# A router that takes four tiles at a time, in a mixture-of-experts kernel that has to be routed first

## The chip, the cores and the metric

The kernel runs on one core of one Trainium2 chip. The metric is the device time of one launch in microseconds (us). The kernel before took 273.12 us as the median of three runs (271.77 to 273.74). The profile shown here is of one further execution.

## The reference, cut to what matters

```python
w = weights[conditions]                      # (32, 64, 64), chosen per sequence
xf = einsum('bct,bcd->bdt', x, w)            # x is (32, 64, 512): 2048 tokens of 512
gate = softmax(xf @ Wr.T)                    # 8 experts
top2_val, top2_idx = top_k(gate, 2)
keep = rank_of_token_within_expert <= 640    # in the order of the tokens
g = silu(xf @ Wg[e].T); u = xf @ Wu[e].T     # 352 wide
y = sum_e comb[:, e] * ((g * u) @ Wd[e].T)
return x + y
```

All tensors are float32. Every token is first mixed with the matrix of its own condition, and then sent to its two best experts, each of which takes at most 640 tokens.

## The kernel before, in words

**Two halves.** The first 42 us find out which token goes to which expert; the rest computes the eight experts. Expert 0 works on tiles of 128 tokens; experts 1 to 7 work on 512 tokens together and on a fifth tile if there is one. Products in the experts are made from a high and a low part of each operand ("high" by ScalarE, `w_high`, `x_high`; "low" by VectorE, `w0_low`, `x_low`).

**The route.** The tokens lie in 16 tiles of 128 (`TT`), in 8 pairs (`NM`), and SyncE (SP) loads a pair with each DMA of 512 KB (`load_x`, L345). The logits are computed as wq^T (x Wr), so the router does not wait for xf. For each tile: TensorE turns four 128x128 blocks of x into one bank (`x_tile_turn`, L1171), VectorE (tiles 1, 2, 5, 6, 9) or ScalarE (the others) copies that bank to a ring of four slots in SBUF, `turned_sb`. For each pair, `router` (L1182) multiplies by Wr, the four blocks of the contraction in four column groups of 32 of the array; VectorE copies the result (`xrT_copy`, L815), TensorE turns it back (`turn`, L1195), and VectorE adds the four parts (`xr_sum`, L820). `logits` (L1210) multiplies by the matrix of the condition, wq, in four groups of tiles, `LG`, of 6, 4, 4 and 2. After each group VectorE finds the two largest of eight (`top_two`, L827). `one_hot` makes the choice a matrix of ones, three small products give each token its rank in its expert (L1269 and L1272), a chain of VectorE steps makes slots of it (L902 to L934), 32 products turn slots into lists of rows (L1283, into `ps_slot`), and VectorE writes the lists (L951, `lists_ok`).

**xf.** `condition(j)` (L1227) computes the rows of xf for a pair, four banks in a ring; ScalarE copies them to `xf_sb` (`xf_copy`, L590), and SP stores each pair to DRAM (L390, L394). Two conditions stand before the last routers, two more before the rank products, four behind them. Then TensorE runs `KEEP_WARM` products whose result nobody reads (L1289).

**The handover.** GpSimd (POOL) gathers the rows of an expert from DRAM by indirect DMA (`gather`, L494). Its first gather waits for `lists_ok` 1 and for `xf_out`, which counts all stores of xf (L485, L486). TensorE turns the gathered tile (`x_turn`, L1296) and starts the first expert (L1385).

**Queues.** SP issues in the order of its text: cond, x pairs 0 and 1, wr, x pairs 2 to 7, two small padding rows, eight `place` DMAs that spread wq (after `wsel_in`), the four gate and up parts of expert 0's weights, the stores of xf, the gates' store, and the down part of expert 0's weights (`load_unit(0, KH)`, L398). Then come the weights of expert 1, each when its part of the buffer is free. The matrices of the other eight tiles come by eight gathers on POOL (L454).

## Time and profile before

| | before |
|---|---|
| median of 3 runs | 273.12 us (271.77 to 273.74) |
| the profiled execution's own time | 272.44 us |
| its span | 270.6 us |
| TensorE busy, whole span | 257.8 us, 95% |
| TensorE busy, 42 to 265 us | 220.3 of 223.0 us |
| VectorE, ScalarE, GpSimd busy | 161.6, 137.7, 173.6 us |
| granted clock of TensorE, mean | 0.991 |
| DMA moved | 59.00 MB |

How to read it: a granted clock of 1.00 is 2.4 GHz, 0.50 is 1.2 GHz. A row of the timeline gives the start of a group of like instructions, how long it lasted from the first start to the last end, and the idle time of its engine before it with what ended that. For an issue on SPq the length is that of the issue, not of the transfer; the landing is a column of the view of DMA issues. A DMA share of 1.00 means that all 16 DMA engines were busy.

### The profile page before, as it was taken

The page shows a single profiled execution, that of the slowest core. Times are in us where ns is not written, and L with a number is a line of the kernel's source. Part 1 is how long each engine was busy: PE and PEld are TensorE (multiplying, and loading weights), DVE is VectorE, ACT ScalarE, POOL GpSimd, SP SyncE. Part 2 cuts the span into 40 slices and gives each one's busy share as a digit, 9 for nine tenths or more (in the row PEclk, how much of TensorE's full clock was granted, in tenths as well). Part 3 has the DMA queues.
Part 4 walks back from the last instruction along what each step waited for, and adds up shares of the span by engine and source line. Part 5 has one row for each costly group of instructions (what it writes and reads, how often), then busy time and mean ns, then how long its engine had stood idle before and what let it go on. Part 6 is the DMA issues. An engine that isn't in the chain of part 4 may idle for free.

```text
span 270.6 us, 4016 instructions
## 1 busy us (share of the span) xinstructions
PE 257.8 (95%) x1368; PEld 200.0 (74%) x1368; DVE 161.6 (60%) x332; ACT 137.7 (51%) x242; POOL 173.6 (64%) x156
## 2 busy tenths in 40 slices
PE   8999698999999999999999999999999999999991
PEld 4663156999987867888878887777787777878980
DVE  2658998444459664876566639674865867343251
ACT  2356843444464656565366644664565559442100
POOL 5792048741158867884887478858887886685742
PEclk9999979999999999999999999999999999999998
DMA  6996888999869998899679867998899699366441
GB/s 201 363 300 241 344 270 272 386 338 330 294 193 209 202 207 256 162 216 277 170 130 250 238 178 111 200 294 251 154 238 329 148 192 225 40 79 81 131 177 46
DMA packets 27099, 59.00 MB, mean 218 GB/s; under 512 B 6198, under 2 KB 6454, under 8 KB 26976
## 3 DMA queue, kind: packets, MB, share of 16 engines
q1 hardware_dynamic: 16416, 37.89, 44.3%
q0 software_dynamic: 10656, 20.75, 37.2%
q8 instruction: 16, 0.26, 0.4%
q14 instruction: 11, 0.09, 0.1%
HBM read 39.56 MB, written 20.25 MB: 221 GB/s over the span
## 4 chain that ended last, share of the span: by engine, by line
PE 52%; DVE 3%; ACT 2%; DMA 2%; issue 2%; POOLq 0%; ACTq 0%; DVEq 0%
PE bank L1342 19%; PE bank L1429 17%; PE bank L1437 9%; PE bank L1316 3%; DMA xg<-xf_dram,src_turn 2%; PE bank L1444 2%; PE bank L1452 2%; DVE w L1005 1%; ACT hhi L696 1%; POOLq L85 0%; DVE squares L1054 0%; PE bank L1303 0%; DVE hlo L1060 0%; DVE h L1120 0%; DVE h_last L1100 0%
## 5 line engine op out<-in xcount | busy, mean ns | idle before, releaser
L1429 PE MATMUL bank<-xhi,w 128*128 128x512 f32 x280 | 71.6, 398 | 0.0
L1342 PE MATMUL bank<-w,hhi 128*128 128x512 f32 (+1 forms) x216 | 67.1, 393 | 1.5 <-ACT y_sb L667 1.0
L554 POOL DMA_INDIRECT out<-y_sb,dst_row x35 | 56.5, 1613 | 13.4 <-issue 13.4
L1429 PEld LDWEIGHTS bank<-xhi,w 128*128 128x128 f32 x280 | 52.3, 188 | 13.2 <-DVE h_last L1100 0.8
L520 POOL DMA_INDIRECT gate_g<-gates_dram,src_row x40 | 46.8, 1170 | 12.1 <-issue 11.5
L1342 PEld LDWEIGHTS bank<-w,hhi 128*128 128x128 f32 x216 | 39.2, 188 | 10.7 <-DVE hlo L1060 1.6
L1005 DVE TENSOR_TENSOR w<-raw,w 128x704 fp32r<-128x704 f32 (+1 forms) x35 | 37.1, 1060 | 14.6 <-ACT w L609 8.2
L508 POOL DMA_INDIRECT xg<-xf_dram,src_turn x24 | 25.6, 1065 | 26.0 <-DVE xlo L990 11.6
L1342 PE MATMUL bank<-w,hlo 128*128 128x512 f32 (+1 forms) x108 | 41.9, 388 | 0.0
L1437 PE MATMUL bank<-xlo,w 128*128 128x512 f32 x140 | 38.4, 396 | 0.0
L609 ACT ACTIVATE w<-raw 128x704 fp32r<-128x704 f32 (+1 forms) x40 | 36.7, 923 | 0.0
L508 POOL DMA_INDIRECT xg<-xf_dram,src_row x16 | 18.1, 1130 | 27.5 <-DMA xf_dram<-xf_sb 15.9
L1054 DVE STREAM_TRANSPOSE squares<-xg 128x512 f32<-128x512 f32 x24 | 24.0, 1046 | 16.7 <-DMA xg<-xf_dram,src_turn 16.7
L1437 PEld LDWEIGHTS bank<-xlo,w 128*128 128x128 f32 x140 | 26.4, 189 | 6.4
L667 ACT ACTIVATE y_sb<-bank,gate_g 128x512 f32<-128x512 f32 x30 | 20.1, 686 | 20.0 <-PE bank L1342 18.6
L1342 PEld LDWEIGHTS bank<-w,hlo 128*128 128x128 f32 x108 | 20.3, 188 | 4.6
L1316 PE MATMUL bank<-w,xhi 128*128 128x352 f32 x112 | 20.5, 327 | 0.8 <-ACT xhi L644 0.8
L1316 PEld LDWEIGHTS bank<-w,xhi 128*128 128x128 f32 x112 | 18.2, 189 | 1.4 <-issue 1.0
L696 ACT ACTIVATE hhi<-h 128x512 fp32r<-128x512 f32 x14 | 8.9, 634 | 19.6 <-DVE h L1107 12.0
L1060 DVE TENSOR_TENSOR hlo<-h,hhi 128x512 fp32r<-128x512 f32 x14 | 9.7, 693 | 10.4 <-ACT hhi L696 10.4
L990 DVE TENSOR_TENSOR xlo<-xg,xhi 128x512 fp32r<-128x512 f32 x24 | 15.0, 684 | 1.5 <-ACT xhi L654 1.5
L654 ACT ACTIVATE xhi<-xg 128x512 fp32r<-128x512 f32 x24 | 13.3, 620 | 2.7 <-DMA xg<-squares 2.7
(138 smaller groups left out, 304.8 us busy)
## 6 DMA issues: line engine op xcount, KB each, us to landing
raw<-wgu SPq DMA_DIRECT2D x32, 352.0 KB, 7.8
xg<-squares SPq DMA_DIRECT2D x24, 256.0 KB, 7.5
x_sb<-x SPq DMA_DIRECT2D x8, 512.0 KB, 7.6
raw<-wd SPq DMA_DIRECT2D x8, 512.0 KB
xf_dram<-xf_sb SPq DMA_DIRECT2D x7, 512.0 KB, 3.0
raw<-wd SPq DMA_DIRECT2D x8, 192.0 KB
out<-x SPq DMA_DIRECT2D x1, 1280.0 KB, 18.3
gate_g<-gates_dram,src_row POOLq DMA_INDIRECT x40, 6.5
```

The lines of the kernel that those rows point to most:

```text
L508: nc.gpsimd.indirect_dma_start(out=xg[:, t, :], out_offset=None, in_=xf_dram[:, :], in_offset=bass.IndirectOffsetOnAxis(ap=rows, axis=0), ...
L520: nc.gpsimd.indirect_dma_start(out=gate_g[:, n % TPE, :], out_offset=None, in_=gates_dram[:, :], in_offset=bass.IndirectOffsetOnAxis(ap=sr ...
L554: nc.gpsimd.indirect_dma_start(out=out[:, :], in_=y_sb[:, n % TPE, :], in_offset=None, out_offset=bass.IndirectOffsetOnAxis(ap=dst_row[:, ...
L609: last = nc.scalar.activation(w[:, half, 0, a:b], raw[:, a:b], ACT.Copy)
L667: nc.scalar.activation(y_sb[:, t, :], y_bank(e, t)[:, :], ACT.Copy, scale=gate_g[:, t, e:e + 1]).then_inc(y_ok, n)
L990: nc.vector.tensor_tensor(xlo4[:, :, cols], turned_rows(e, t), xhi4[:, :, cols].bitcast(F32), ALU.subtract).then_inc(xlo_ok, n)
L1005: last = nc.vector.tensor_tensor(w[:, half, 1, a:b], raw[:, a:b], w[:, half, 0, a:b].bitcast(F32), ALU.subtract)
L1054: nc.vector.transpose(squares[:, :, t, :], xg[:, t, :].rearrange("p (i b) -> p b i", i=SQ)).then_inc(squares_ok, 1)
L1316: last = nc.tensor.matmul(ps[:, 0:I], left[:, b, c], w[:, half, part, o:o + I], start=(k == 0 and left is xhi and part == 0), stop=(k == K ...
L1342: last = nc.tensor.matmul(ps[:, cols], left(c), w[:, half, part, o:o + width], start=(c == 0 and q == 0), stop=(closes and c == cs[-1] and ...
L1429: last = nc.tensor.matmul(ACC_BANK[what][:, :], columns(what, k, part), xhi4[:, k, :], start=(k == 0 and part == 0), stop=False)
L1437: last = nc.tensor.matmul(ACC_BANK[what][:, :], columns(what, k, 0), xlo4[:, k, :], start=False, stop=(k == KH - 1))
```

## The change

The router works on four tiles instead of two (`router(g)`, g 0 to 3), in a ring of twelve slots `turned_x`, with products 512 columns wide; the copies of the results of groups 2 and 3 are made by ScalarE, and group 3 has banks 2 and 3 for itself. The last two tiles of x are loaded a second time, already turned (`xt`, 512 KB, prepared as another input); their blocks are not turned on TensorE, nor copied. x pair 7, needed only for xf, is loaded after the `place` DMAs, and so are the padding rows. The groups of logits are 4, 4, 4 and 4 tiles. All conditions come after the last logits, two ahead of the rank products and six behind. All softmax work is done once, the sums between the slots and the lists, the last product after the lists. The down part of expert 0's weights is loaded ahead of the stores of xf. Its high part is made before `x_high(0)`, its low part before `x_low(0)`; all low parts of gate and up come after the lists; the copies to `src_turn` come after `x_low(0)`. `KEEP_WARM` goes from 18 to 25.

```diff
-LG = ((0, 3), (3, 5), (5, 7), (7, NM))
+LG = ((0, 2), (2, 4), (4, 6), (6, NM))
-KEEP_WARM = 18
+KEEP_WARM = 25
-        ps_xrT, ps_xr = bank[6:8]
+        ps_xrT = (bank[6], bank[6], bank[6], bank[2])
+        ps_xr = (bank[7], bank[7], bank[7], bank[3])
+        XRT_DVE = 2
# SP
-            for m in range(2, NM):
+            for m in range(2, NM - 1):
                 load_x(m)
-            (the two padding rows)
+            sp.dma_start(turned_x[:, RING:RING + 2, :, :], xt...).then_inc(xt_in, 16)
             for j in range(HALF, TT):
                 place(j)
+            load_x(NM - 1)
+            (the two padding rows)
-            for u in range(KH):
+            for u in range(NU):
                 load_unit(0, u)
             (the stores of xf, the store of the gates)
-            load_unit(0, KH)
# ScalarE
-            (xf_copy of 16 tiles, exps after 2 and 6 of them, w_high(0) after 4)
+            for g in range(XRT_DVE, NG):
+                act.wait_ge(xrT_ps, g + 1)
+                nc.scalar.activation(xrT[:, g % 2, :], ps_xrT[g][:, :], ACT.Copy).then_inc(xrT_ok, 1)
+            for n in range(TT):
+                xf_copy(n, n % XR)
+                if n == TT - 3:
+                    act.wait_ge(sub_ok, 2)
+                    nc.scalar.activation(ex[:, :, :], lg[:, :, :], ACT.Exp).then_inc(ex_ok, 1)
+            w_high(KH, 0, 0)
             x_high(0)
-            w_high(KH, 0, 0)
# VectorE
+            for j in TURN_DVE[0:4]:
+                turn_copy(j)
+            xrT_copy(0)
+            for j in TURN_DVE[4:]:
+                turn_copy(j)
+            xrT_copy(1)
+            xr_sum(0)
+            xr_sum(1)
+            top_two(0)
+            top_two(1)
+            xr_sum(2)
             one_hot(0)
+            xr_sum(3)
+            top_two(2, 3)
             subtract(LG[3][0] * 2, TT)
             one_hot(1)
+            subtract(0, LG[3][0] * 2)
...
+            w0_low(KH)
             x_low(0)
-            w0_low(KH)
+            (the 16 copies to src_turn)
# TensorE
             router(g):
+                        for half, r in enumerate((turned_slot(g * XR), RING)):   # g == 3, for each k
+                            cols = slice(half * 2 * P, (half + 1) * 2 * P)
+                            last = nc.tensor.matmul(ps_xrT[g][k * Q:(k + 1) * Q, cols], wr_sb[:, k, :], turned_x[:, r:r + 2, k, :])
+            turn_tiles(0, 8)
+            pe.wait_ge(wr_in, 16)
+            router(0)
+            turn_tiles(8, 12)
+            router(1)
+            turn(0)
+            turn_tiles(12, TURNED)
+            turn(1)
+            logits(0)
+            router(2)
+            logits(1)
+            router(3)
+            turn(2)
+            turn(3)
+            logits(2)
+            logits(3)
+            condition(0)
+            condition(2)
             (the rank products)
-            for j in range(after, TT, 2):
+            for j in range(4, TT, 2):
                 condition(j)
# first expert
-                    pe.wait_ge(wlo0_ok, KH)
+                    pe.wait_ge(wlo0_ok, 2)
...
+                if s == 0:
+                    pe.wait_ge(wlo0_ok, KH)
                 first_gate_up(s, n, (2, 3))
```

## Rows read from the trace of the kernel before

**Rows 1.** Busy time in stretches: start:end, length, engines, granted clock, DMA share, GB/s
```profile
0.00:42.00 42.00, 37.52 (x335) 19.35 (x335) 29.15 (x127) 20.39 (x36) 20.27 (x33) 0.96 0.83 283
42.00:265.00 223.00, 220.32 (x1033) 180.65 (x1033) 132.27 (x206) 117.35 (x206) 152.25 (x123) 1.00 0.83 210
```

**Rows 2.** Waits of TensorE from 78 to 265 us: total, times, longest
```profile
PE bank L1342 <- ACT y_sb L667: 1.0, 1, 1.0
PE bank L1342 <- DVE hlo L1060: 0.5, 1, 0.5
```

**Rows 3.** Timeline at the handover: start, length, engine, line, what, idle before
```profile
37.55 1.73 POOL L508 DMA_INDIRECT xg<-xf_dram,src_row  x1 [15.88 <-DMA xf_dram<-xf_sb]
...
36.08 5.75 PE L1289 MATMUL bank<-iota_q 128*128 128x512 f16 x18
42.09 0.63 PE L1303 MATMUL bank<-ident,xg 128*128 128x128 f32 x4 [0.26 <-DMA xg<-xf_dram,src_row]
43.49 1.50 PE L1316 MATMUL bank<-w,xhi 128*128 128x352 f32 x8 [0.78 <-ACT xhi L644]
```

**Rows 4.** Issues of xf's stores, first and last: timeline, and us from issue to landing
```profile
23.23 0.33 SPq L390 DMA_DIRECT2D xf_dram<-xf_sb  x1
...
xf_dram<-xf_sb SPq DMA_DIRECT2D x1, 512.0 KB, 2.6
...
33.49 0.85 SPq L394 DMA_DIRECT2D xf_dram<-xf_sb  x1
...
xf_dram<-xf_sb SPq DMA_DIRECT2D x1, 256.0 KB, 3.3
```

**Rows 5.** Timeline of VectorE, the route's last steps
```profile
26.86 0.38 DVE L845 TENSOR_TENSOR ohp<-iota_e,i 128x128 bf16<-128x128 f32 x1
27.92 0.70 DVE L902 TENSOR_TENSOR_SCAN run<-carry,bank 128x264 f32<-128x264 f32 x1
36.29 0.20 DVE L951 TENSOR_SCALAR src_row<-bank 128x40 uint32<-128x40 f32 x1
39.92 3.41 DVE L974 COPY src_turn<-src_row 32x6 uint32<-32x6 uint32 x16
```

**Rows 6.** Busy time in stretches, DMA share and GB/s last: loads, idle, stores
```profile
3.00:22.00 19.00, 18.46 (x190) 11.32 (x188) 9.70 (x47) 6.25 (x11) 15.64 (x23) 1.00 1.04 333
22.00:23.00 1.00, 1.00 (x18) 0.42 (x18) 0.86 (x7) 0.88 (x2) 0.00 (x0) 1.00 0.15 59
28.00:30.00 2.00, 1.71 (x16) 0.30 (x8) 1.90 (x4) 1.24 (x4) 0.00 (x0) 1.00 1.00 406
```

**Rows 7.** Timeline of TensorE and VectorE in the router's stretch
```profile
14.59 1.04 PE L1178 MATMUL bank<-ident,x_sb 128*128 128x128 f32 x8
15.56 0.64 PE L1190 MATMUL bank<-turned_sb,wr_sb 128*32 128x256 f32 x8
16.13 0.44 PE L1201 MATMUL bank<-ident,xrT 128*128 128x128 f32 x2
20.73 0.41 PE L1223 MATMUL bank<-xr,wq 64*64 64x8 f32 x16
20.99 1.07 PE L1234 MATMUL bank<-x_sb,wq 64*64 64x512 f32 x8
21.21 0.39 DVE L832 MAX8 v<-bank 128x8 f32<-128x8 f32 x4
...
22.34 0.24 DVE L864 TENSOR_TENSOR lg<-bank,v 128x80 f32<-128x80 f32 x1
```

**Rows 8.** Issue and us to landing of x pair 7, last of the x loads
```profile
5.42 0.64 SPq L348 DMA_DIRECT2D x_sb<-x  x1
...
x_sb<-x SPq DMA_DIRECT2D x1, 512.0 KB, 12.0
```

**Rows 9.** Copies of xf by ScalarE, timeline
```profile
31.40 2.06 ACT L593 ACTIVATE xf_sb<-bank 128x512 f32 x4 [0.32 <-PE bank L1234]
```

**Rows 10.** Busy time and granted clock in the two stretches after 36.8 us
```profile
36.80:40.20 3.40, 3.40 (x10) 1.19 (x9) 3.28 (x10) 0.22 (x2) 2.34 (x2) 0.50 0.70 207
40.20:43.60 3.40, 2.37 (x13) 1.08 (x12) 3.16 (x16) 0.85 (x2) 2.52 (x3) 1.00 0.67 173
```

More of the change, by code:

```diff
@@ L39 @@
 AQ = 8
[L40 to L44 removed]
+LG = ((0, 2), (2, 4), (4, 6), (6, NM))
+NG = len(LG)
+RING = 3 * XR
+TURNED = TT - 2
 WARM_UP = 10
[L47 removed]
+KEEP_WARM = 25
 BASE = TPE - 1
@@ L279, in build, with turned_slot @@
         TURN_DVE = [1, 2, 5, 6, 9]
-        TURN_ACT = [j for j in range(TT) if j not in TURN_DVE]
+        TURN_ACT = [j for j in range(TURNED) if j not in TURN_DVE]
+        def turned_slot(j):
+            return j % RING if j < TURNED else RING + j - TURNED
         def group_of(j):
@@ L943, in w0_low @@
                                         ALU.subtract).then_inc(wlo0_ok, 1)
-            for u in range(W0_EARLY):
-                w0_low(u)
+            gate_sums()
             dve.wait_ge(slot_ps, 1)
@@ L1203, in turn @@
+                last.then_inc(xrT_ps, 1)
+            def turn(g):
+                pe.wait_ge(xrT_ok, g + 1)
+                if 1 <= g < NG - 1:
+                    pe.wait_ge(xr_ok, g)
+                for j in range(XR):
+                    last = nc.tensor.transpose(ps_xr[g][:, j * P:(j + 1) * P],
+                                               xrT[:, g % 2, j * P:(j + 1) * P], ident[:, :])
                 last.then_inc(xr_ps, 1)
```

193 lines of the change are left out of this document (73 added, 120 removed).

## The prediction

> **What bounds the kernel now.** I read the stretches first. From 42 to 265 us TensorE is busy 220.3 of 223.0 us at full clock, and before that only 37.5 of 42 [rows 1]. Its waits in the experts come to 1.5 us in all from 78 us on [rows 2]. The change touches no product of experts 1 to 7. So the end stands at a nearly fixed distance behind the first expert's first tile turn, at 42.09 [rows 3], and the question is what moves that.
>
> The timeline at the handover says who holds it. TensorE's filler products end at 41.83, and the turn waits 0.26 us for a gathered tile; the gather was issued by POOL at 37.55, and POOL had been released by a store of xf [rows 3]. Two things have to be there: the lists, whose first write runs 36.29 to 36.49 [rows 5], and all stores: the last is issued at 33.49 and lands 3.3 us later, at 36.8 [rows 4]. The stores decide, but the lists are only 0.3 us ahead. Whoever makes the route faster alone gains nothing, and whoever makes the stores faster alone gains 0.3 us.
>
> What do the stores hang on? The first is issued at 23.23 and lands in 2.6 us [rows 4]. While they flow freely the 16 DMA engines are full at 406 GB/s, and from 22 to 23 us they are nearly empty, since the loads are through [rows 6]. All of xf is 8 x 524 KB; at 406 GB/s a pair takes 1.29 us and the eight 10.3. The fixed part of a store is 2.6 - 1.3 = 1.3 us. A stream that never runs dry would have landed at 23.23 + 1.3 + 10.3 = 34.9; it landed at 36.8, so 1.9 us were gaps behind ScalarE, whose copies share the time with routers, exps and a weight part.
>
> **The route, part by part.** A tile pair's turns take 1.0 us, a router of 256 columns 0.57 (15.56 to 16.13), a turn back of two blocks 0.27, eight quadrant products of logits 0.26, and the two largest of four tiles 1.13 on VectorE (21.21 to 22.34) [rows 7]. A 512-column router is not in the trace. At least the streaming part doubles, at most all of it: 0.9 to 1.14, I take 1.05. The router's work on TensorE is thus the same as before; what goes is one pair of tile turns (1.0) and half of the handshakes.
>
> I let tiles 10 and 11 be turned when they were, at 14.59 [rows 7], since the loads up to there stay as they are. From 15.6: router(1) 1.05, turn(0) 0.5, tiles 12 and 13 1.0, turn(1) 0.5, logits(0) 0.3, router(2) 1.05, which is 20.0. logits(1) waits for top_two(0), which starts near 19.0 and takes 1.13: 20.1, ends 20.4. router(3) needs xt. It takes the place in the queue of x pair 7, which landed at 5.42 + 12.0 = 17.4 [rows 8], so it is hidden by 3 us. It ends at 21.4; ScalarE's copy takes 0.6 (four in 2.06 [rows 9]) and a handshake: 22.1. turn(3) 0.5, VectorE's sum 0.4, logits(3) 0.3: condition(0) starts at about 23.4. It started at 20.99 before [rows 7].
>
> VectorE has eight tiles to do behind that (2.1 us from 23.2), then a subtraction and the second one_hot (0.38 [rows 5]): 25.9, against 26.86 + 0.38 = 27.24. The gates no longer stand between it and the scan. The scan goes from 27.92 to about 26.5, and since w0_low(0) is behind the lists now, the whole chain with the slots moves with it: lists at about 35.0, 1.4 us earlier. That is the change's gain, and alone it buys nothing.
>
> **The stores.** Before, condition(0) at 20.99 gave a first issue at 23.23, 2.24 us on. Now 23.4 + 2.2 = 25.7. The queue in front of them grows by xt (0.52 MB) and the down part (0.72 MB). Loads ended near 22.1, and 1.25 MB at the mean rate of the loads, 333 GB/s [rows 6], are 3.7 us: 25.8. The two meet. From 25.7 a full stream lands at 25.7 + 1.3 + 10.3 = 37.3. ScalarE's pace is 1.03 us a pair [rows 9], below 1.29, so it keeps ahead, but for one place: the rank products stand between condition(2) and condition(4) and wait for one_hot until 25.9. Pair 3 is then issued at about 28.6 where the stream wants it at 28.3: 0.3 us. Stores landed: 37.6, against 36.8. The 1.9 us of gaps are given back, but the later start takes 2.4 and the new gap 0.3: +0.8.
>
> Bounds of this term: if everything waits only on the DMA queue, packets run from 25.8 to 36.1 and the landing is between 36.1 and 37.4: -0.7 to +0.6. If router(3) runs in series (below), +1.8.
>
> The Trainium skill, DMA: Bandwidth & Descriptors, section on bandwidth, gives about 358 GB/s as what one core gets of its HBM in transfers between HBM and SBUF. By that the stores would take 11.7 us and the sum be 1.4 larger; the measured 406 GB/s speaks against it here, and the sum uses 406.
>
> **Moves at no cost, and their cover.** The padding rows and pair 7 on SP (0.5 to 1.6 us of issue each) go behind the places: the weights are issued later, but the engines still have places and pair 7 to work on, and ScalarE wants no weight before 33. The place DMAs stay where they were in time, and logits(3) came at 24 already. gates' store is behind the lists, near 36.5; POOL needs it only after five gathers. The down part's high and low products (1.5 and 1.8 us) leave the stretch behind the handover, but TensorE did not wait for them: from 43.49 it runs on [rows 1, 3]. They fit before 42. The 16 copies to src_turn, 3.41 us [rows 5], now stand between x_low(0) and x_low(1). x_low(0) ends 2.0 us behind the tile turn, the copies 5.4, x_low(1) 6.1; TensorE asks for it 7.0 behind the turn. Hidden by 0.9 us; if that cover is gone they cost what exceeds it. The length of the filler is weighed in rival B.
>
> **Sum.** POOL's first gather and all behind it move by +0.8: 272.44 + 0.8 = 273.2. The profiled execution is 0.7 below the median of 273.12, so against the median this is +0.1. I forecast 273.2, no change that can be measured; 1% (2.7 us) is about what a measurement of this kernel can tell.
>
> **Rival A: the stores end earlier.** If conditions start by 22.5, or the loads drain faster, the queue decides and the stores land at 36.1 to 36.5; the lists at 35.0 are no hindrance, where before they would have been. Time 271.7 to 272.1. For: pair 5 of x was surely there before 14.59. Against: the chain of router(3), a copy, a turn, a sum and logits(3) has no slack. Even this is not 1%: that would need the stores at 34.1, and 4.19 MB behind loads that end at 25.8 do not get there. What would make it faster by over 1% is that a gather lands sooner than the 4.4 us of now as well.
>
> **Rival B, slower: TensorE's clock falls under the first expert.** The filler starts at 34.7 and has 25 products. Before, 18 took 5.75 us, 3.4 of them at half clock [rows 3, 10], which is 4.05 us at full, 0.225 each. So 25 take 5.6 us: they end at 40.3, and the tile is there at 42.9. Before, the wait was 0.26 us [rows 3]; now it is 2.6, and then 0.8 for xhi. The trace shows one fall to 0.50, from 36.8 to 40.2, after TensorE had waited for slots and done 32 products of 40 columns [rows 10]. If the new idle time brings such a fall, 3.4 us at half clock under the experts cost 1.7: 274.9. Two such stretches cost 3.4: 276.6. It passes 1% above the median (275.85) once 5.3 us are run at half clock. Against: if the clock falls under the filler as before, the filler lasts until 42.0 and no gap is left. The Trainium skill, TensorE: Matmul & The Clock Gate, Part 1, has the throttled clock as the default that only activity releases, which is the same rule; the trace agrees with it in its one fall.
>
> **Rival C: router(3) is in series.** It issues, for each of the four blocks, both halves of the columns, and neighbours then share a column group. If half a product waits for its neighbour, it takes up to 2.1 instead of 1.05, all on the path of the stores: 274.3. The Trainium skill, same page, Part 3, says that matmuls start and end strictly in order, which would give this. No row of before has such an order.
>
> **Numbers.** Forecast 55% (272.5 to 274.0), A 15%, B 17% (a third of it over 1%), C 8%, the rest 5%, unknown on both sides. The spread of the three runs, 2 us, and A make the low end 271.5; C and one fall of the clock make the high end 275.3. Faster by over 1%: 5%; within 1%: 84%; slower: 11%.
>
> **What would show it.** The scan near 26.5 and lists near 35; condition(0) near 23.4, the first store near 25.7, DMA engines full from there on, with the last store landing at 37.6; POOL's first gather near 38.3, still released by a store; TensorE idle some 2.6 us ahead of the first tile turn at 42.9, and its clock from there on; router(3) of 1 or of 2 us. The forecast is wrong if the gather is released by the lists, if the stores land before 36, or if TensorE waits for x_low(1) or a weight part in the first expert.

## The result, and the profile after

The changed kernel takes 276.62 us, median of four runs (275.50 to 277.63), against 272.50 for the kernel before beside it: ratio 1.0146, 95% interval 1.0086 to 1.0205. Timed once more (six runs, below), it took 277.06 against 273.18: 1.0156 (1.0111 to 1.0200). So it is 1.5% slower, where 273.2 and "no change" had been forecast. Here and below a median is of all runs of a kernel, and a ratio leaves out the runs that are more than 1.5% above the fastest of their kernel, so the two need not agree.

Its profiled execution took 277.63 us, with a span of 275.9: 5.2 us more than before (272.44). First the same two stretches as [rows 1] with the half-clock stretches behind them, and TensorE's waits as in [rows 2], but from 42 us on, of the changed kernel:

```profile
0.00:42.00 42.00, 36.19 (x310) 19.16 (x310) 25.86 (x104) 21.67 (x36) 17.90 (x32) 1.00 0.84 287
42.00:265.00 223.00, 217.97 (x1003) 178.92 (x1004) 130.86 (x210) 115.41 (x204) 152.56 (x120) 0.98 0.83 206
43.80:47.20 3.40, 2.10 (x7) 1.76 (x8) 1.11 (x3) 0.60 (x1) 2.75 (x4) 0.50 0.75 186
47.20:50.60 3.40, 3.40 (x15) 3.33 (x14) 3.11 (x15) 0.00 (x0) 2.63 (x4) 0.50 1.03 405
```
```profile
PE bank L1306 <- DMA xg<-xf_dram,src_row: 2.9, 1, 2.9
PE bank L1345 <- DVE hlo L1043: 0.9, 1, 0.9
PE bank L1434 <- DVE h_last L1083: 0.9, 2, 0.5
PE bank L1319 <- ACT xhi L642: 0.8, 1, 0.8
```

Two things are new: a wait of 2.9 us for the first gathered tile, and two stretches in a row at half clock, 43.8 to 50.6, that is under the first expert. The half-clock stretch of before, in the filler [rows 10], is gone. The timeline at the handover answers to [rows 3]:

```profile
40.21 1.47 POOL L519 DMA_INDIRECT xg<-xf_dram,src_row  x1 [18.58 <-DMA xf_dram<-xf_sb]
...
33.41 2.57 PE L1286 MATMUL bank<-pick_t,turned_sb 128*128 128x40 f16 x32
35.80 5.58 PE L1292 MATMUL bank<-iota_q 128*128 128x512 f16 x25
44.32 1.09 PE L1306 MATMUL bank<-ident,xg 128*128 128x128 f32 x4 [2.94 <-DMA xg<-xf_dram,src_row]
46.18 0.63 PE L1319 MATMUL bank<-w,xhi 128*128 128x352 f32 x1 [0.78 <-ACT xhi L642]
```

The filler ends at 41.38; the first tile turn comes at 44.32 instead of 42.09 [rows 3]. I split the 5.2 us there and at the first 512-wide product of expert 1's gate and up (83.28 after, 78.50 before). Up to the first turn: +2.23. From it to expert 1: 38.96 against 36.41, +2.55. From there to the end: 192.62 against 192.10, +0.5, less than two executions of one kernel differ by (193.32 in e16 and 191.47 in e15, the same two kernels once more, below). The middle term begins with the clock: the wait for xhi is 0.78 as before, but four tile turns take 1.09 us instead of 0.63 [rows 3].

The first and the last stores, as in [rows 4] (each landing stands under its issue), and the route on VectorE as in [rows 5]:

```profile
25.47 0.35 SPq L402 DMA_DIRECT2D xf_dram<-xf_sb  x1
...
xf_dram<-xf_sb SPq DMA_DIRECT2D x1, 512.0 KB, 3.8
...
35.29 0.80 SPq L406 DMA_DIRECT2D xf_dram<-xf_sb  x1
...
xf_dram<-xf_sb SPq DMA_DIRECT2D x1, 256.0 KB, 4.2
```
```profile
25.24 0.38 DVE L841 TENSOR_TENSOR ohp<-iota_e,i 128x128 bf16<-128x128 f32 x1
...
26.31 0.70 DVE L895 TENSOR_TENSOR_SCAN run<-carry,bank 128x264 f32<-128x264 f32 x1 [0.52 <-issue]
...
31.28 2.49 DVE L923 TENSOR_TENSOR turned_sb<-iota_q,slot_tp 128x1024 f16<-128x1024 f16 x4
...
36.09 0.20 DVE L941 TENSOR_SCALAR src_row<-bank 128x40 uint32<-128x40 f32 x1 [1.65 <-PE bank L1286]
```

The scan came at 26.31 (26.5 forecast) and the first store at 25.47 (25.7). The last store landed at 35.29 + 4.2 = 39.5, where 37.6 was forecast, and the lists came at 36.09, where 35.0 was. The next rows show TensorE in the router's stretch, as [rows 7]:

```profile
20.01 1.09 PE L1189 MATMUL bank<-turned_x,wr_sb 128*32 128x256 f32 x16
21.03 0.66 PE L1201 MATMUL bank<-ident,xrT 128*128 128x128 f32 x4
21.84 0.66 PE L1201 MATMUL bank<-ident,xrT 128*128 128x128 f32 x4 [0.16 <-ACT xrT L617]
22.43 0.96 PE L1223 MATMUL bank<-xr,wq 64*64 64x8 f32 x32
23.20 1.53 PE L1235 MATMUL bank<-x_sb,wq 64*64 64x512 f32 x12
...
31.41 2.07 PE L1235 MATMUL bank<-x_sb,wq 64*64 64x512 f32 x16 [0.31 <-ACT xf_sb L604]
```

router(3), whose neighbours share a column group, took 1.09 us for its 16 products: not in series. The first condition came at 23.20 (23.4); the last ones wait for ScalarE's copies and end at 33.4.

The DMA engines in the stretch of the stores, share and GB/s last. First the loads, then the stores' stream from the first issue, its full part, its end, and all of it:

```profile
17.00:22.00 5.00, 4.57 (x71) 2.70 (x70) 2.73 (x28) 2.28 (x4) 4.62 (x5) 1.00 0.86 208
...
25.50:37.00 11.50, 10.56 (x89) 5.03 (x90) 8.90 (x28) 9.50 (x19) 0.00 (x0) 1.00 0.98 381
37.00:39.50 2.50, 2.50 (x14) 1.09 (x12) 2.46 (x6) 2.47 (x4) 0.00 (x0) 1.00 0.40 145
...
25.50:39.50 14.00, 13.06 (x101) 6.12 (x102) 11.37 (x33) 11.97 (x22) 0.00 (x0) 1.00 0.88 339
```

From 25.5 to 39.5 they moved 14.0 x 339 = 4.75 MB: 4.19 of stores and 0.5 that the loads had left over. Until 37.0 they were full; the last 0.36 MB (2.5 x 145), 0.9 us of work at 406 GB/s, took 2.5, at a mean share of 0.40. I call these 1.6 us the tail. They are close to the 1.9 between 37.6 and 39.5, but that is partly luck: the left-over loads, which the sum did not have here, filled the 1.3 us that it had set aside as the fixed part of a store. e3 (below), without them, is the clean case.

### The profile page after: what moved, and what is told of

Read it like the earlier page. It is cut to its first block, busy times and chain, and to the rows that moved or that the text cites. A ratio compares the mean times of both kernels' runs of the same rounds, so it can differ in the third digit from the quotient of the medians.

```text
span 275.9 us, 3919 instructions
## 1 busy us (share of the span) xinstructions
PE 259.1 (94%) x1343; PEld 202.3 (73%) x1343; DVE 159.7 (58%) x318; ACT 137.6 (50%) x241; POOL 175.7 (64%) x156
## 3 DMA queue, kind: packets, MB, share of 16 engines
q0 software_dynamic: 10656, 20.75, 36.8%
## 4 chain that ended last, share of the span: by engine, by line
PE 60%; DVE 12%; DMA 10%; ACT 7%; issue 6%; SPq 1%; POOL 1%; POOLq 1%; DVEq 0%; ACTq 0%
PE bank L1345 19%; PE bank L1434 14%; PE bank L1319 11%; PE bank L1442 7%; DMA xg<-xf_dram,src_turn 4%; DMA x_sb<-x 4%; DVE w L988 3%; DVE squares L1037 3%; PE bank L1306 2%; PE bank L1235 2%; ACT hhi L694 2%; ACT w L624 2%; ACT xf_sb L604 2%; DMA xf_dram<-xf_sb 2%; DMA xg<-xf_dram,src_row 1%
## 5 line engine op out<-in xcount | busy, mean ns | idle before, releaser
L565 POOL DMA_INDIRECT out<-y_sb,dst_row x35 | 57.5, 1642 | 14.5 <-issue 10.4
L531 POOL DMA_INDIRECT gate_g<-gates_dram,src_row x40 | 47.9, 1197 | 12.1 <-issue 10.9
L519 POOL DMA_INDIRECT xg<-xf_dram,src_turn x24 | 25.7, 1070 | 24.2 <-DVE xlo L973 9.2
L1442 PE MATMUL bank<-xlo,w 128*128 128x512 f32 x140 | 38.4, 396 | 0.0
L1037 DVE STREAM_TRANSPOSE squares<-xg 128x512 f32<-128x512 f32 x24 | 24.6, 1055 | 17.2 <-DMA xg<-xf_dram,src_turn 17.2
L1319 PE MATMUL bank<-w,xhi 128*128 128x352 f32 x112 | 21.7, 341 | 0.8 <-ACT xhi L642 0.8
L1319 PEld LDWEIGHTS bank<-w,xhi 128*128 128x128 f32 x112 | 19.3, 199 | 1.6 <-issue 1.1
```

Of the source, the lines that this page charges most:

```text
L519: nc.gpsimd.indirect_dma_start(out=xg[:, t, :], out_offset=None, in_=xf_dram[:, :], in_offset=bass.IndirectOffsetOnAxis(ap=rows, axis=0), ...
L531: nc.gpsimd.indirect_dma_start(out=gate_g[:, n % TPE, :], out_offset=None, in_=gates_dram[:, :], in_offset=bass.IndirectOffsetOnAxis(ap=sr ...
L565: nc.gpsimd.indirect_dma_start(out=out[:, :], in_=y_sb[:, n % TPE, :], in_offset=None, out_offset=bass.IndirectOffsetOnAxis(ap=dst_row[:, ...
L1037: nc.vector.transpose(squares[:, :, t, :], xg[:, t, :].rearrange("p (i b) -> p b i", i=SQ)).then_inc(squares_ok, 1)
L1319: last = nc.tensor.matmul(ps[:, 0:I], left[:, b, c], w[:, half, part, o:o + I], start=(k == 0 and left is xhi and part == 0), stop=(k == K ...
L1442: last = nc.tensor.matmul(ACC_BANK[what][:, :], columns(what, k, 0), xlo4[:, k, :], start=False, stop=(k == KH - 1))
```

## The experiments

All are edits of the kernel before or after; line numbers as there. "T0" is the first tile turn, "T0 to expert 1" the second of the three stretches above. Ratios are to the kernel before, timed beside each kernel on the same chip; run times of kernels from different chips are compared by their ratios alone.

### The clock: e1, e18, e6

```diff
# e1_filler38 and e18_filler38_again: the changed kernel
-KEEP_WARM = 25
+KEEP_WARM = 38
# e6_before_filler8: the kernel before
-KEEP_WARM = 18
+KEEP_WARM = 8
```

> The changed kernel with 38 filler products instead of 25, nothing else. In the changed kernel the filler ended at 41.4 us, the first tile turn came at 44.3, and the clock stood at 0.50 from about 43.9 to 50.3. Theory (the idle time brings the fall): the filler lasts to about 44.2, the stores and the gather stay where they are (gather 40.2), the clock stays at 1.00 under the first expert, and the time falls by some 3.4 us, to 273 to 274. Rival (the fall comes from the slot products or from another cause): the half-clock stretch stays, at the filler or the expert, and the time stays at 276 to 277.

> The kernel before with 8 filler products instead of 18, nothing else. Its filler then ends at about 38.5 and TensorE is idle for some 3.5 us ahead of the first tile turn, as it was for 2.9 in the changed kernel. Theory (idle time ahead of the experts costs half-clock time under them): the handover stays at 42.1, the clock is at 0.50 for 3.4 to 6.8 us from 42 to 50, the time is 1.7 to 3.4 us above the kernel before. Rival (the filler does nothing for the clock of the experts): no half-clock stretch behind 43, time unchanged.

> The kernel e1_filler38 once more (the changed kernel with 38 filler products instead of 25), whose profiled execution had no stretch at half clock and took 273.65 us, but whose median of four was 275.68. Theory (the half-clock stretches under the first expert are worth their 1.7 us each): median 1.7 to 2.5 us below e15_after_again of the same chip. Rival (the longer filler delays the first tile turn in the executions in which the stores land early, or the clock falls elsewhere): median within 1 us of e15_after_again.

e1's TensorE in the two stretches in which the changed kernel ran at half clock (busy, then granted clock), and then e6's in its first half-clock stretch under the expert, with its wait:

```profile
43.80:47.20 3.40, 2.53 (x16) 2.17 (x16) 1.78 (x6) 0.60 (x1) 2.75 (x4) 1.00 0.79 226
47.20:50.60 3.40, 3.40 (x24) 3.38 (x23) 3.14 (x14) 1.06 (x2) 2.63 (x4) 1.00 1.03 391
```
```profile
42.18 1.08 PE L1303 MATMUL bank<-ident,xg 128*128 128x128 f32 x4 [3.01 <-DMA xg<-xf_dram,src_row]
...
41.70:48.50 6.80, 5.54 (x21) 5.13 (x21) 4.20 (x11) 1.97 (x2) 5.69 (x6) 0.50 0.92 308
```

With the filler up to the turn, the clock stays at 1.00, and T0 to expert 1 takes 36.45 us, as before (36.41); the profiled execution takes 273.65. And the kernel before, with its filler cut, stands idle for 3.01 us, runs 6.8 us at 0.50 behind it, and needs 38.96 for that stretch. The other profiles (their edits are below) line up by how long the clock stood at half behind T0:

| at half clock behind T0 | T0 to expert 1 | TensorE idle ahead of T0 | executions |
|---|---|---|---|
| none | 36.37 to 36.48 us | 0 to 0.26, 1.67, 1.80 | before, e1, e9, e10, e12, e13, e18; e14; e17 |
| 3.4 us | 37.94 to 38.04 | 1.82, 2.25, 2.51, 2.90, 2.93, 2.96 | e4, e11, e8, e5, e2, e3 |
| 6.8 us | 38.96 to 39.17 | 2.88, 2.94, 3.01 | e15, the changed kernel, e6 |

Two stand outside, both at full clock: e16 (37.70) and e7 (37.33), which wait 1.1 and 0.6 us for a later gathered tile. So the 2.55 us are the clock. It was not one execution's chance either: of the changed kernel's ten, nine have a mean granted clock of 0.980 to 0.986, and the tenth, 0.992, is its fastest (275.50); with 38 filler products all sixteen have 0.987 to 0.998.

In the times less of it is seen. e1: 275.68 us, 1.0069 (1.0002 to 1.0135). e18: 276.17, 1.0097 (1.0058 to 1.0137), beside 277.06 for the changed kernel on the same chip: 0.9 us by the medians, 1.6 by the ratios, with intervals that overlap. e6: 275.07, 1.0049 (1.0007 to 1.0090), 1.3 us. The two profiles shown are the ends of their kernels: e1's was its fastest run, e6's its slowest of ten. And more varies than the clock: at a mean clock of 0.997 or 0.998 the runs with 38 filler products lie between 273.87 and 278.11 us, and in the profiles the rest, expert 1 to the end, takes from 191.4 to 194.4. The theory "1.7 to 2.5 us below" did not come true for e18's median, the rival's "within 1 us" did.

### The queue of SP: e2, e3, e4, e7

```diff
# e2_down_late, e7: the changed kernel
-            for u in range(NU):
+            for u in range(KH):
                 load_unit(0, u)
             (the stores of xf)
+            load_unit(0, KH)
# e3_pads_early, e7: the changed kernel, the two padding rows behind xt,
# ahead of the place DMAs; e7_queue_as_before also has KEEP_WARM = 30
# e4_before_down_early: the kernel before
-            for u in range(KH):
+            for u in range(NU):
                 load_unit(0, u)
             (the stores of xf)
-            load_unit(0, KH)
```

> The changed kernel with the down part of expert 0's weights loaded behind the last store of xf again. Theory (the load ahead of the stores delays them): 0.72 MB leave the queue, at 370 to 208 GB/s 1.9 to 3.4 us; the last store lands at 36.8 to 37.6 instead of 39.5, the first gather starts at 37.5 to 38.3, the first tile turn comes at 41.9 to 42.7, and since the filler ends at 41.4 the clock does not fall: 272 to 273. Rival (the later first store, at 25.5, holds it): the last store lands at 38.5 or later and less than 1 us comes back from it.

> The changed kernel with the two padding rows issued ahead of the place DMAs again, pair 7 still behind them. In the changed kernel the DMA engines moved 208 GB/s from 17 to 22 us, before 289 from 16 to 22. Theory (the padding rows, 1.3 us of issue between pair 7 and the weights, starve the queue): the rate of that stretch goes to 280 or more, the loads end 1 to 2 us earlier, the last store lands at 38 to 38.5 instead of 39.5. Rival (the order of pair 7 and the weights, or something in the memory, slows it): rate and landing stay within 0.4 us.

> The kernel before with the down part of expert 0's weights loaded right behind the gate and up parts, ahead of the stores; nothing else. Its loads then end at about 24.1 instead of 22.1, its first store is issued at 23.2, and its stream of stores has 1.9 us of gaps. Theory (the stream takes up a late start only as far as it has gaps): the last store lands 0 to 0.5 us later than 36.8, time 272.5 to 273. Rival (every microsecond of load ahead of the stores moves them): last store at 38.7, the filler of 18 too short by 2 us, time 274.5 and more with a fall of the clock.

> The changed kernel with both orders of the queue undone, the down part behind the last store and the padding rows ahead of the places, and 30 filler products. The route stays the changed one. Theory: nothing is queued ahead of the stores, which start at 25.5 and flow; last store lands at 37.5 if no engine is late, at 39.0 if the instruction packet at 33.5 to 34 still delays one; gather at 37.9 or 39.4, the filler bridges to 42, time 272.5 to 274.5. Rival (the later start of the stores alone costs the whole difference): gather at 40 and the time stays above 276.

e3 is the one that separates. Its loads, its stream up to 37.0, its tail, two parts of the tail, and then its first store and its last:

```profile
17.00:22.00 5.00, 4.58 (x72) 2.71 (x70) 2.74 (x27) 2.28 (x4) 4.56 (x5) 1.00 1.07 346
...
25.50:37.00 11.50, 10.49 (x91) 4.87 (x92) 9.28 (x30) 10.01 (x19) 0.00 (x0) 1.00 0.90 355
37.00:39.50 2.50, 2.50 (x14) 1.13 (x12) 2.50 (x5) 2.47 (x4) 0.00 (x0) 1.00 0.25 85
...
37.40:38.00 0.60, 0.60 (x5) 0.26 (x3) 0.60 (x2) 0.60 (x1) 0.00 (x0) 1.00 0.09 31
38.60:39.20 0.60, 0.60 (x4) 0.28 (x3) 0.60 (x2) 0.60 (x1) 0.00 (x0) 1.00 0.07 25
```
```profile
25.51 0.35 SPq L402 DMA_DIRECT2D xf_dram<-xf_sb  x1
xf_dram<-xf_sb SPq DMA_DIRECT2D x1, 512.0 KB, 2.6
...
35.42 0.46 SPq L406 DMA_DIRECT2D xf_dram<-xf_sb  x1
xf_dram<-xf_sb SPq DMA_DIRECT2D x1, 256.0 KB, 4.1
```

The loads went at 346 GB/s instead of 208 and were through before the first store (share 0.11 from 25.0 to 25.5), which landed in 2.6 us instead of 3.8. Up to 37.0 the prediction's form holds: 4.08 MB are 10.1 us of work at 406 GB/s, and with the fixed part of 1.3 that is 11.4 of the 11.5 us. But the last store still landed at 39.5: the last 0.21 MB took 2.5 us, 2.0 more than their bytes. So the leftover loads, which I had priced as meeting the stores, did not hold the end by themselves. What is left at the end are the rows of about one engine: a share of 0.07 and 25 GB/s from 38.6 to 39.2, where a sixteenth of 406 is 25 (in between, from 38.0 to 38.5, the small store of the gates ran).

e3 took 278.14 us, 1.0159 (1.0122 to 1.0195). e2, with the down part behind the stores, 276.38, 1.0090 (1.0035 to 1.0144), last landing 39.4; e7, both at once and a filler of 30, 276.58, 1.0115 (1.0042 to 1.0188), last landing 38.8. The other way round, the kernel before with the down part ahead of its stores: 273.96, 0.9999 (0.9941 to 1.0058). In its profile the gather came at 39.53 and T0 at 43.74, but the whole route was late there, from a wait of 1.48 us for x at 10.72 on: its first condition started at 22.76 (before: 20.99), its first store 2.24 behind that, as before, and its last store landed at 38.8, 2.0 later than before. The order of the queue is not the main part of what the change costs; up to 1.5 us of it these intervals can't rule out.

### Where the conditions stand: e10, e8, e11, e13

```diff
# e10_before_conditions_late: the kernel before, all conditions behind the logits
+            router(7); turn(6); turn(7); logits(2); logits(3)
             condition(0)
             condition(2)
             (the rank products, then the other six)
# e8_early_condition: the changed kernel with e2 and e3's queue, e5's small
# products (below), KEEP_WARM = 27, condition(0) and its two copies early
             router(2)
+            condition(0)
             logits(1)
# e11_early_conditions: e8, a third condition ahead of the ranks, KEEP_WARM = 28
+            condition(4)
# e13_early_conditions_filler37: e11
-KEEP_WARM = 28
+KEEP_WARM = 37
```

> The kernel before with its conditions moved as in the change: none ahead of the last logits, two ahead of the rank products, six behind (exps(0) ahead of the first copy, which this needs). Router, queue and filler of 18 stay. Theory (the stores start with the conditions, and the rest of the DMA time is fixed): route 1 to 2 us earlier, condition(0) at 22.3 to 22.8, first store at 24.6 to 25 instead of 23.2, last store at 37.5 to 38 or later, gather at 38 to 39 and the time 1 to 2 us above the kernel before. Rival (the place of the conditions is paid back, since the gaps of the stream close): gather at 37.6 or earlier, no change in time.

> As the last one, and with it the 55 small products of the shift, the first pair of xf computed and copied ahead of the second group of logits, and 27 filler products. Theory: the first store is issued at 21.7 instead of 25.5, so that the stores have slack of over 1 us and no longer decide; the rank products come some 0.7 us later, near 26.4; lists at 36.5 to 37 and gather at 36.8 to 37.3; with the filler ending near the first tile turn at 41.5 no half-clock stretch follows; time 271.5 to 272.5, below the kernel before by 0.5 to 1 us. Rival (the stores stay bound by the queue or by a late engine): gather at 38.5 or later, no gain on the kernel before.

> As the kernel with an early first pair, 55 small products and the queue's orders undone, and now also condition(4) ahead of the rank products, where TensorE was idle for 1.4 us; 28 filler products. Theory: pairs 0 to 2 of the stores go out by 27, the stream has no gap left from 28 on, the last store lands at 36.4 to 37, lists at 35.5 to 36, gather at 36.9 to 37.4, first tile turn at 41.5, time 271.5 to 273, at or just below the kernel before. Rival (ScalarE's pace and an instruction packet hold the last store): last store at 38.5 and no gain over the version before it, 276 to 277.

> The kernel e11_early_conditions with 37 filler products instead of 28. Its first tile turn was at 43.4 and its clock was at 0.50 for 3.4 us under the first expert (44.7 to 48.1). Theory: 9 more products of 0.22 us leave no idle time ahead of the first tile turn, no stretch at half clock stands under the first expert, T0 to expert 1 falls from 37.95 to about 36.4, the first tile turn is still at 43.3 to 43.6, and the time is 1 to 1.7 us below the 274.55 measured there, near 273. Rival (the clock falls anyway, later, or the filler delays the turn): unchanged within 0.5 us or slower.

e10 puts the one property "conditions late" into the kernel before: 275.96 us, 1.0095 (1.0058 to 1.0132). Its first store was issued at 27.04 and its last landed at 39.5, T0 45.34. It is not a clean copy: TensorE ran at 0.50 from 23.5 to 26.9, which made its conditions slower, and again for 6.8 us from 37 on, so that the filler reached up to T0, 5.1 us behind the gather where the others have 3.6 to 4.8: up to 1 us of its later T0 may be the filler. Without a tail (the end of its stream: share 0.90, 285 GB/s) its stream took 12.5 us:

```profile
38.50:39.50 1.00, 1.00 (x12) 0.72 (x11) 0.94 (x4) 0.99 (x2) 0.00 (x0) 0.50 0.90 285
```

e11 goes the other way: the new router with its conditions early again. 274.55 us, 1.0013 (0.9984 to 1.0042): level with the kernel before. e7, with the same order of the queue and late conditions, had 1.0115, an interval that only touches this one (1.0042). One condition moved early (e8) was not enough, 277.32, 1.0133 (1.0073 to 1.0194). The profile does not show where e11 gains: its first store, issued at 21.50, landed at 28.3, behind the loads; its last, issued at 33.60, took 5.2 us and landed at 38.8, as late as e7's; T0 is 0.26 earlier than e7's (43.38 and 43.64), and the rest of the difference between these two executions lies behind expert 1's start, where executions of one kernel differ as much. In e11 the filler ended at 41.13 and TensorE stood idle for 2.25 us ahead of T0, with 3.4 us at half clock behind it. e13 took that away (gather 38.01, T0 42.76, T0 to expert 1 36.42, no stretch at half clock), and yet came to 275.16, 1.0042 (1.0002 to 1.0081). Here the filler that mends the profile did not show in the ratio at all.

### The tail of the stores: e5, e12, e15, e16

In the changed kernel and in e1, e2 and e3, one 16 KB packet of the instruction queue stood in the stream, at 33.4 to 34.0. The kernel before has its packets at 26.0 and 36.8. The row below is of the changed kernel, 33.8 to 35.0 us, packets, MB and share of 16 engines' time, which is 0.9 us of one engine:

```profile
q8 instruction: 1, 0.02, 4.8%
```

Each store is spread over all engines (in the kernel before, with only the first one under way, the share from 24.4 to 25.0 us is 0.96), so one engine with other work might hand in its rows last. e5 shifts the packets by other instructions of TensorE; e12 puts 2 x 16 KB of other work into the stream of the kernel before.

```diff
# e5_shift_fetch: the changed kernel
-WARM_UP = 10
+WARM_UP = 5
+            for _ in range(55):   # ahead of the second group's logits
+                nc.tensor.matmul(bank[4][0:Q, 0:Q], warm[:, 0:Q], warm[:, 0:Q], start=True, stop=True)
# e12_before_side_traffic: the kernel before, behind the store of pair 4
+                if m == 4:
+                    sp.dma_start(side[:, :], x[0:16, :]...).then_inc(side_out, 16)
```

> The changed kernel with five of the ten warm-up products replaced by 55 small ones (32x32), so that TensorE's program has 100 more instructions ahead of the route. In the changed kernel a 16 KB instruction packet is read at 33.9 us, in the middle of the stores; from 37.4 to 39.2 us one DMA engine alone (share 0.06 to 0.1, 25 GB/s) still stores rows, and the last store lands at 39.5. Theory (that packet sits on one of the 16 engines, whose rows then come last): the packet moves to 26 to 29 us, where the stream of stores still has a gap, the tail of one engine goes, the last store lands at 37.8 to 38.3 and the gather starts at 38.2 to 38.7 instead of 40.2; time 1 to 1.5 us less, about 275. Rival (one engine is slow by itself, or the packet belongs to another engine's program): the tail stays at 39.2, gather at 40 or later, time 276.6.

> The kernel before, with one more DMA of 2 x 16 KB, from one DRAM tensor to another, issued by SP between the stores of pair 4 and pair 5 of xf (near 30.1 us); nothing waits for it but the end. Theory (one DMA engine that has 16 KB of other work in the middle of the stream of stores finishes its rows of the stores last, since every store is spread over all engines): the last store, which landed 3.3 us behind its issue at 33.49, lands 4.2 to 5 behind, near 37.8 to 38.5, with one or two engines alone at work at its end, POOL's first gather starts at 38.3 to 39.0 instead of 37.5, and the time is 0.5 to 1.5 us above that of the kernel before. Rival (the stream shares the engines evenly, and the late landing in the changed kernel comes from its own length and the stalls of issue): the landing stays within 0.4 us of 36.8, and the gather starts at 37.5 to 38.0.

> The changed kernel itself, once more, for a second profiled execution. In the first its last store landed 4.2 us behind its issue, at 39.5, and POOL's first gather began at 40.21. In e14_before_fetch_late45 the stores were issued as in the kernel before and still landed 5.1 us behind the issue (gather 39.45). Theory (how long the last store takes varies from execution to execution by up to 2 us, whatever the kernel; what the change adds by itself is its later first issue): the last issue is at 35.3 again, and the landing is somewhere from 38.2 to 40; gather 38.6 to 40.5. Rival (the changed order makes it late each time): landing 39.2 to 39.8 again. Time by either 275.5 to 277.6, median near 276.6, ratio 1.008 to 1.015.

> The kernel before itself, once more, for a second profiled execution and as the measure of chance. Theory (the landing varies between executions): gather anywhere from 37.4 to 39.6. Rival (the kernel before lands its stores at 36.8 each time): gather 37.4 to 37.8. Ratio 1.000 within 0.004 by either: whatever it is off from 1 is what chance does to the ratios of the other kernels.

e5's packets moved to 27.8 and 37.4, and its last store was no earlier: gather 41.46, 277.96 us, 1.0112 (1.0028 to 1.0197), with a tail again. (The 55 products also made its route and its first store, at 26.83, 1.4 us later; from there to the last landing it took 13.9 us, as in the changed kernel, 14.0.) The first row is of 38.4 to 40.0 in e5. e12's side traffic landed where it was meant to, and the stores ended as in the kernel before; then its gather:

```profile
38.40:40.00 1.60, 1.60 (x9) 0.77 (x8) 1.60 (x4) 1.59 (x3) 0.00 (x0) 1.00 0.25 73
```
```profile
30.09 0.54 SPq L395 DMA_DIRECT2D side<-x  x1
...
side<-x SPq DMA_DIRECT2D x1, 32.0 KB, 2.8
...
37.37 1.54 POOL L514 DMA_INDIRECT xg<-xf_dram,src_row  x1 [15.79 <-DVE dst_row L972]
```

The profile names `dst_row` as what released that gather, but it raises the same semaphore as the lists, for whose first value the gather waits, besides the stores. e12: 273.87 us, 0.9983 (0.9941 to 1.0025). The theory falls for work at 30 us; the stream still had slack there (270 GB/s from 30 to 31), so engines could catch up, and work in the full part of the stream was not tried.

The second execution of the changed kernel repeats the first: the tail of the stream, the handover and the two half-clock stretches.

```profile
37.00:39.10 2.10, 2.10 (x11) 0.93 (x10) 2.10 (x3) 2.09 (x3) 0.00 (x0) 1.00 0.31 108
...
39.86 1.22 POOL L519 DMA_INDIRECT xg<-xf_dram,src_row  x1 [18.29 <-DMA xf_dram<-xf_sb]
...
43.66 0.82 PE L1306 MATMUL bank<-ident,xg 128*128 128x128 f32 x4 [2.88 <-DMA xg<-xf_dram,src_row]
...
44.00:47.40 3.40, 2.62 (x10) 2.25 (x9) 2.17 (x8) 0.60 (x1) 2.65 (x4) 0.50 0.82 234
47.40:50.80 3.40, 3.40 (x14) 3.34 (x14) 2.03 (x11) 0.60 (x1) 2.61 (x3) 0.50 1.04 412
```

Its last store was issued at 34.95 and landed 4.2 later, at 39.1. The kernel before repeats itself as well: gather 37.76, T0 41.88, no tail (share 0.91 from 36 to 37), 272.97 us, 0.9997 (0.9965 to 1.0028). The kernel before with 45 small products (e14, below) had a late landing too: share 0.35 and 92 GB/s from 36.5 to 37.0, last store 5.1 us, gather 39.45, although its stores are issued as in the kernel before.

The twenty profiles, taken together, speak for the packets after all. The table sets the start of the packet nearest to the last store's issue against how long that store took to land:

| packet, against the last store's issue | last store, issue to landing | executions |
|---|---|---|
| 2.2 us ahead to 2.6 us behind | 3.8 to 5.2 us | the changed kernel, e1, e2, e3, e5, e7, e8, e11, e14, e15, e18 |
| 3.0 to 3.5 us behind | 3.3 to 3.8 | before, e4, e9, e12, e13, e17 |
| 5.8 us or more away | 3.4 to 3.6 | e6, e10, e16 |

e5 did not take the packet out of the stream: it moved the next one in, 1.7 us behind the last issue. And e14 did what e9 (below) was made for: against e9 it has twenty more small products ahead of its packet, which comes at 36.2 instead of 36.8, and its last store took 5.1 us instead of 3.4. This is no proof. The table was made after the fact, all executions of its first line but e14 have the new router, and the only one with the new router outside it is e13 (3.8). The tail does not go with the place of the conditions: the last store took 5.1 and 5.2 us in e8 and e11, where they are early, and 3.5 in e10, where they are late. Nor does it go with a late last issue alone: in the changed kernel the last store is issued 0.94 us behind the one before it, at 35.29, and in the kernel before 0.49, at 33.49; but e2, which issues it at 34.37, 0.54 behind, landed at 39.4 all the same. So what makes the tail is not settled; the packet in the last microseconds of the stream is the candidate that all twenty profiles leave standing.

### TensorE's idle time ahead of the slots: e9, e17, e14

```diff
# e9_before_fetch_late, e17_before_fetch_late_again: the kernel before; e14: 45
+            for _ in range(25):   # behind the last conditions, ahead of the slots' products
+                nc.tensor.matmul(bank[4][0:Q, 0:Q], iota_q..., iota_q..., start=True, stop=True)
```

> The kernel before with 25 small products (32x32, their result unused) put between the last condition and the slot products, where TensorE is idle for 1.5 us. Nothing else waits on them; they only move TensorE's instruction packet, which is read at 36.8 us behind the last store in the kernel before, forward into the stores. Theory (a 16 KB packet holds one DMA engine for 1 us and its rows come last): the packet comes at 33 to 34.5, one engine stores alone for 1 us or more at the end, the last store lands at 37.8 to 38.5 instead of 36.8, the gather starts at 38.3 to 39 instead of 37.6. Rival (the packet does not matter): last store 36.8 to 37.2, gather 37.5 to 38.

> The kernel e9_before_fetch_late once more (25 small products ahead of the slots), which came to 0.9959 (0.9932 to 0.9987) of the kernel before, while 45 products gave 1.0011. Theory (a real gain of 25 products): ratio 0.994 to 0.998 again. Rival (chance): 0.998 to 1.004.

> The kernel e9_before_fetch_late with 45 small products instead of 25 ahead of the slots' products. With 25 it was faster than the kernel before (ratio 0.9959, 0.9932 to 0.9987). Theory (activity in TensorE's idle time ahead of the slots is what helped, by keeping the clock): the stretch at half clock, 36.2 to 39.6 there, gets shorter or goes, the first tile turn stays at 41.8 to 42.1, and the ratio is 0.993 to 0.998. Rival 1 (e9's gain was chance): ratio 0.998 to 1.002. Rival 2 (45 products last beyond the moment at which the slots are ready, and delay the lists): lists 0.3 to 0.8 us later, ratio 1.000 to 1.003.

The packet at 36.8 stayed where it was, so e9 did not test what it was made for. But it was faster, twice, by a little: 272.67 us, 0.9959 (0.9932 to 0.9987), and 272.52, 0.9973 (0.9950 to 0.9996). The wait for the slots fell from 1.50 us to 0.78. The rows are of e9's TensorE, then of e17's, whose clock stayed up even there:

```profile
31.97 0.79 PE L1280 MATMUL bank<-iota_q 128*32 128x32 f16 x25
33.54 2.56 PE L1286 MATMUL bank<-pick_t,turned_sb 128*128 128x40 f16 x32 [0.78 <-DVE turned_sb L930]
```
```profile
35.94 4.06 PE L1292 MATMUL bank<-iota_q 128*128 128x512 f16 x18
41.80 0.63 PE L1306 MATMUL bank<-ident,xg 128*128 128x128 f32 x4 [1.80 <-DMA xg<-xf_dram,src_row]
...
40.00:45.00 5.00, 2.42 (x16) 2.24 (x16) 4.21 (x17) 1.97 (x2) 4.04 (x5) 1.00 0.72 197
```

What it gains I can't show from the profiles: T0 is at 41.77 and 41.80, against 42.09 and 41.88 in the two of the kernel before, which is 0.1 to 0.3 of the 0.7 to 1.1 us. With 45 products it is gone: 1.0011 (0.9969 to 1.0054), and a median of 275.82 for its twelve runs, 1.65 above that of the kernel before beside it. Its profile (276.48 us) has the late last store shown above, with T0 at 43.61.

## Why the prediction was wrong, by its own steps

Two terms of the sum failed: the landing of the stores came out 1.5 to 1.9 us later than forecast, and the wait ahead of the first turn, put at nothing, cost 2.55 us through the clock.

**The route: right.** condition(0), the second one_hot, the scan and the first store came within 0.3 us of the forecast, the 512-column router took 1.07 to 1.09 (1.05 taken), and rival C fell: neighbours in one column group did not wait for each other. The Trainium skill, TensorE: Matmul & The Clock Gate, Part 3, has matmuls start and end strictly in order. The prediction read from this that router(3) would take up to 2.1 us; the 1.09 does not bear that reading out.

**The lists: wrong, and without effect.** They came 0.2 us earlier than before (0.8 in e15), not 1.4. The forecast moved the whole chain with the scan. VectorE did its part: the first of its four picks for the slots starts at 31.28, where before it was 32.89. But on TensorE the slots' products stand behind six conditions, which wait for ScalarE's copies until 33.4, and start there. Before, they had waited 1.50 us for VectorE and started near 33.7. It costs nothing as long as the stores decide, as they did here.

**The landing of the stores: the step that was mis-sized.** "From 25.7 a full stream lands at 37.3", 0.3 more for one gap: 37.6. Measured 39.5 and 39.1. The start was right. The form "fixed part plus bytes at the full rate" fails at the end of the stream: from 37.0 on the engines worked at a share of 0.40, which cost 1.6 us (1.5 in the second execution: 2.1 us for 0.23 MB, and 2.0 in e3) that no row of before had. Two of my inputs were off besides: the loads did not end at 25.8 (the last part of the weights landed at 21.24 + 8.1 = 29.3), since they flowed at 208 GB/s from 17 to 22 us, not 333; and full stores ran at 381 to 404. ScalarE kept ahead, as forecast: the third pair was issued at 28.91 (28.29 in the second execution; 28.6 forecast), and its copies went on at 1.19 us a pair, slower than the 1.03 taken but faster than the 1.29 of the stores. e3 shows that the leftover loads alone did not hold the end. The gaps of ScalarE, 1.9 us before, were indeed given back: e3's stream up to 37.0 is full but for the fixed part. So the term that was mis-sized is the end of the stream; why it ends so late stays open, with the packet of instructions as the candidate that the profiles leave.

**The clock: the step that was put at nothing, and the rival that happened.** The likeliest case let the turn wait 2.6 us at no cost. The wait was 2.94 and 2.88, and both executions had two half-clock stretches behind it. Rival B had priced exactly that, two stretches, at 3.4 us and 276.6; it cost 2.55 in the profile, since TensorE was busy for only 5.5 of these 6.8 us. I gave rival B 17%, and a third of that to over 1%. My ground against it, that the clock would fall in the filler as before, came from one profile of before. What it rested on was likely the idle time of 1.50 us ahead of the slots, which the change removed: in none of the eleven profiles with the new router does the clock fall there, in seven of the nine with the old one it does. But that this wait brings the fall is not shown: e4 has the 1.50 us and no fall in the filler, and with 0.78 us e9 has one and e17 none. The Trainium skill, TensorE: Matmul & The Clock Gate, Part 1, has the throttled clock as the default which only activity releases. The traces of the changed kernel, e1 and e6 agree; in e17 and e7 TensorE idled 1.80 and 1.83 us and kept its clock.

**The sum.** +0.8 was forecast. In the profiles it is +5.2: the first turn +2.23 (0.8 forecast, and the landing 1.9 later than that, less 0.4 because the first gather took 4.1 us to the turn instead of 4.5), the clock +2.55, +0.5 not assigned. In the medians it is +3.9 to +4.1. The median of e18, which has the turn at 44.13 and full clock, is 3.0 above the kernel before (2.6 by the ratio), where the two turns are 2.0 to 2.3 apart; up to 1 us of that has no place in the profiles.

## What to carry to other kernels

When an engine has to be kept busy up to a handover, the length of the filler must follow the transfer that ends the wait, with the worst landing seen; take the clock's fall as part of the cost of each wait that a change lengthens, at the place where it will then stand. Expect less of it in the median than in the profile (1.6 us of 2.55 in e18, none in e13). Price a stream of stores with its end, not by bytes at the full rate: what is waited for are the last rows, and here they came 1.5 to 2.0 us behind what their bytes need. Look for other work of a single DMA engine, such as the 16 KB packets of instructions, in the last microseconds of such a stream. And a chain is not earlier because its head is: look for what now stands ahead of each later link on its engine.

## What the runs showed of the hardware

- The place of two transfers of 2 KB in the queue of SP (the padding rows, DRAM to DRAM) may matter for the loads around them, but this is not settled. With them between the place DMAs and the weights, the engines moved 208 to 308 GB/s from 17 to 22 us in six executions; with them ahead of the place DMAs, 346 and 338 in e3 and e7, but 249, 253 and 277 in e8, e11 and e13.
- TensorE's idle time ahead of the first turn, and its clock behind it: up to 0.26 us and after 1.67, 1.80 and 1.83 (e14, e17, e7) it kept 2.4 GHz, after 1.82 (e4) and 2.25 to 2.96 (e11, e8, e5, e2, e3) it ran 3.4 us at 1.2 GHz, and after 2.88, 2.94 and 3.01 (e15, the changed kernel, e6) 6.8 us. The length of the wait alone does not decide between 3.4 and 6.8. The 3.4 us cost 1.5 to 1.6 us, the 6.8 us 2.5 to 2.8.
- From its issue to its landing the last 256 KB store took 3.8 to 5.2 us in the eleven executions in which a 16 KB packet of the instruction queue started between 2.2 us ahead of that issue and 2.6 behind it, and 3.3 to 3.8 in the nine others. Such a packet held one engine for 0.9 to 1.8 us. That it is the cause was not tested.
- The same program varies by 2 to 7 us from run to run (271.68 to 275.86 in twelve runs of the kernel before, 272.02 to 279.32 in twenty-four on another chip), so one profile per kernel, as e1's, can be 2 us off its median.
